# Attention over 13 key tiles in six steps a head instead of seven: the last step multiplies three tiles' values

## What is computed

```python
# wide layer
logits = jnp.einsum('bhqd,bhkd->bhqk', q, k) * scale      # 16 heads, d = 64
probs = jax.nn.softmax(logits + col_bias[None, None, :, :], axis=-1)
out = jnp.einsum('bhqk,bhkd->bhqd', probs, v)
out = out.transpose(0, 2, 1, 3).reshape(B, HW, HEADS * HEAD_DIM) @ Wo + bo + residual
# narrow layer
qg = q.reshape(B, T, N_KV_HEADS, n_rep, HEAD_DIM)         # 4 groups, d = 16
attn = softmax(jnp.einsum('btgrd,bsgd->bgrts', qg, k) * scale)
out = residual + jnp.einsum('bgrts,bsgd->btgrd', attn, v).reshape(B, T, -1) @ wo
```

## Time and profile before

| | |
|---|---|
| runs | median 4529.59 us, 4527.27 to 4530.70 (3 runs) |
| profiled execution | 4529.87 us; its span 4528.1 us, so 1.8 us lie outside the span |
| PE matmuls busy | 4472.1 us, 99% |
| DVE, POOL, ACT busy | 68%, 63%, 51% |
| mean granted clock of PE | 0.991 |
| one wide head | 62 us, and 69 us where an output is projected |
| one narrow head | 39.7 us, and 46 us with a projection |

### The profile page before, as it was taken

How to read it: one execution, slowest core, us unless ns; L and a number is a source line. 1 busy time by engine, 2 the same in 40 slices (tenths; PEclk the granted TensorE clock), 3 DMA queues, 4 the chain that set the end, 5 groups by cost and what they waited for, 6 DMA issues and landing times.

```text
span 4528.1 us, 56837 instructions
## 1 busy us (share of the span) xinstructions
PE 4472.1 (99%) x20621; PEld 2825.6 (62%) x20621; DVE 3067.4 (68%) x5034; ACT 2308.4 (51%) x4123; POOL 2836.3 (63%) x1375
## 2 busy tenths in 40 slices
PE   9999999999999999999999999999999999999999
PEld 8889756666566455555565666666656666666664
DVE  4222567777777687788646777777766677777776
ACT  3322555555555446666654555455555554555453
POOL 0000479888988700111047889888975798889886
PEclk9999999999999989999999999999999999999999
DMA  5565822122212111011151222122216221222120
GB/s 193 181 204 183 276 64 62 44 64 70 66 48 49 36 23 16 12 15 17 57 191 39 63 65 70 45 68 66 56 47 205 64 68 38 64 69 69 45 49 30
DMA packets 125850, 349.61 MB, mean 77 GB/s; under 512 B 29238, under 2 KB 47158, under 8 KB 114619
## 3 DMA queue, kind: packets, MB, share of 16 engines
q1 hardware_dynamic: 125568, 345.98, 28.8%
HBM read 191.38 MB, written 120.31 MB: 69 GB/s over the span
## 4 chain that ended last, share of the span: by engine, by line
PE 94%; DVE 4%; issue 1%; DMA 1%; ACT 0%; POOL 0%; DVEq 0%; SPq 0%; ACTq 0%
PE ST L1098 14%; PE SS L1079 13%; PE ST L1099 12%; PE OA L1109 12%; PE OB L1109 11%; PE ST L1255 5%; PE OA L1263 4%; PE SS L1241 3%; DVE acc L1757 2%; PE OB L1241 1%; PE SS L1118 1%; PE ST L1174 1%; PE ST L1175 1%; PE ST L1176 1%; PE SS L1145 1%; PE SS L1146 1%
## 5 line engine op out<-in xcount | busy, mean ns | idle before, releaser
L958 POOL TENSOR_TENSOR acc<-acc,P 128x1024 f32<-128x1024 f32 x912 | 2215.9, 2461 | 304.2 <-DVE acc L1763 291.1
L1472 ACT ACTIVATE P<-ST 128x512 f32<-128x512 f32 (+1 forms) x2496 | 1464.3, 597 | 1259.8 <-PE ST L1099 1133.6
L1736 DVE TENSOR_REDUCE mpart<-SS 128x1 f32<-128x400 f32 (+1 forms) x3072 | 1629.0, 569 | 666.4 <-PE SS L1079 590.5
L1098 PE MATMUL ST<-QX,KX 128*128 128x512 f32 (+1 forms) x2496 | 1024.7, 411 | 5.6 <-DMA QS<-mrow 3.7
L1099 PE MATMUL ST<-QS,KS 69*128 69x512 f32 (+1 forms) x2496 | 990.2, 397 | 0.0
L1079 PE MATMUL SS<-KS,QS 68*128 68x400 f32 (+1 forms) x3072 | 976.7, 352 | 7.8 <-DVE xacc L1787 2.8
L1079 PEld LDWEIGHTS SS<-KS,QS 68*128 68x128 f32 x3072 | 583.2, 190 | 183.7 <-DVE xacc L1787 26.1
L1098 PEld LDWEIGHTS ST<-QX,KX 128*128 128x128 f32 (+1 forms) x2496 | 464.2, 186 | 361.9 <-issue 274.8
L1109 PE MATMUL OA<-P,Vp 128*64 128x512 f32 (+1 forms) x2496 | 658.3, 606 | 0.0
L1109 PE MATMUL OB<-P,Vp 128*64 128x512 f32 (+1 forms) x2496 | 641.3, 592 | 0.0
L1583 ACT ACTIVATE PG<-ST 128x512 f32<-128x512 f32 (+1 forms) x832 | 425.9, 618 | 202.0 <-PE ST L1255 201.8
(11 more groups left out here) (259 smaller groups left out, 4442.5 us busy)
## 6 DMA issues: line engine op xcount, KB each, us to landing
q_parts<-stq SPq DMA_DIRECT2D x96, 512.0 KB, 5.2
QX<-q_parts SPq DMA_DIRECT2D x96, 512.0 KB, 11.2
KX<-k_parts SPq DMA_DIRECT2D x48, 801.0 KB, 9.3
QS<-q_parts SPq DMA_DIRECT2D x45, 512.0 KB
R<-R SPq DMA_DIRECT2D x360, 64.0 KB, 2.0
v_tiles<-sv SPq DMA_DIRECT2D x24, 832.0 KB, 5.9
Vp<-v_tiles SPq DMA_DIRECT2D x24, 832.0 KB, 7.1
k_parts<-skh SPq DMA_DIRECT2D x48, 400.5 KB, 4.8
```

Of the source, the lines that this page charges most:

```text
L958: gp.tensor_tensor(out, out, P[0:k, slot(H, t), q, :], ALU.add).then_inc(pool_a, 1)
L1098: pe.matmul(bank, KX[H % 2][:, t * 128:t * 128 + k], QX[H % 2][:, q], start=True, stop=False)
L1472: act.activation(P[0:k, slot(H, t), j, :], ST[n % 3][0:k, :], ACT.Exp, scale=SCALE).then_inc(act_p, 1)
L1736: dve.tensor_reduce(mpart[H % 2][:, i // len(KCH), c:c + 1], SS[RING_AT["s", H, i] % 3][:, 0:w], AX.X, ALU.max).then_inc(dve_ss, 1)
```

## The change

One line of the tables. Before, `PV` is 0-1, 2-3, 4-5, 6-7, 8-9, 10-11, 12: seven steps. After, it is 0-1, 2-3, 4-5, 6-7, 8-9, 10-11-12: six steps. So STEPS goes from 7 to 6, ROW_STEP from 5 to 4, and BEFORE_ROW (units ahead of the row's step) from 40 to 32. No instruction of computation is added or dropped.

```diff
-PV = [range(t, min(t + 2, KT)) for t in range(0, KT, 2)]
+PV = [range(t, t + 2) for t in range(0, KT - 3, 2)] + [range(KT - 3, KT)]
 STEPS = len(PV)
 ROW_STEP = STEPS - 2
 BEFORE_ROW = sum(len(PV[g + 1]) for g in range(ROW_STEP)) * JQ
```

## The result

The changed kernel takes 4545.3 us (median of 6 runs, 4539.24 to 4548.1), the kernel before in the same comparison 4528.4 (6 runs). The ratio is 1.0037, with a 95% interval of 1.0027 to 1.0047: slower by 0.37%, 17 us. The forecast was 4536, "no change that can be told, on its slow side"; 4545.3 lies inside its range of 4524 to 4548, but the interval excludes 1, so a change can be told, which the forecast had denied. The profiled execution took 4548.1 us, its span 4546.3, so the two traces differ by 18.2 us.

What follows compares the result with a forecast made beforehand. PE, busy 99% of the span and holding 94% of the chain, was taken as the bound. Wide layers -6.5 and narrow layer +12.8 gave +6.3 us on the profiled 4529.87, forecast 4536, range 4524 to 4548.

Steps and rivals of the forecast that it cites:

- The blocks: Wide heads: each block of values has 0.34 us of overhead, which one block fewer gives back; a block of three takes 5.30.
- the dense steps: First heads: DVE binds; wide steps of 16 S tiles take 7.8 us (+4.45 a layer), narrow ones of 14 6.06 (+4.8).
- the transfer: Narrow head 6: head 8's queries land no earlier, so PE waits 6.3 us for them, net +5.8.
- Rival 1: Only the blocks count and the two waits might hide: -24 us, 4506; chance 0.08.
- rival 2: DVE's ring of S-tile banks binds every narrow 12-unit step: 4548 to 4560, about 4550; chance 0.17.
- Head 15, with two blocks merged, gains 0.2 to 0.3: Last head of each wide layer: merging two blocks makes it 0.2 to 0.3 us shorter.
- Usual wide heads: Wide heads 1 to 13: each gains 0.34 us, 13.3 us over the three layers.
- Nothing new waits there: Wide heads 1 to 13: DVE's 14 S tiles take 7 us beside the 12 units' 8.47, so no new wait.
- Head 6's clock term: Narrow head 6: low clock behind PE's wait costs +1.3 to +3.0 us, taken as 2.2.
- Narrow head 14: It loses S tiles but its units go at ACT's pace; heads 14 and 15 put at 0 (-0.7 to +2).
- Rival 3: Head 6's low clock lasts through the step, three wide first heads lose 1.5 us more each: 4542; chance 0.13.
- A wide layer: Sum of its heads: -4.4 + 4.45 - 1.95 - 0.25 = -2.2 us, the three layers -6.5.

Runs made afterwards that it cites:

- The half reduction: Changed kernel, but DVE takes the maxima of each layer's second head over only half of each S tile's columns: 4528.3 us, ratio 0.9998.
- the early split: Changed kernel, but POOL splits the queries of narrow heads 8 to 15 ahead of head 5's division, not behind it: 4538.0 us, ratio 1.0016.
- the kernel with the step of three at 8 to 10: Six steps as in the changed kernel, but tiles 8-10 form the step of three and 11-12 the last: 4537.4 us, ratio 1.0017 to the kernel before.
- the second five-step kernel: Changed kernel with five steps (tiles 0-1, 2-3, 4-6, 7-9, 10-12), both POOL edits and 12 early S tiles: 4813.4 us, ratio 1.0623.

## Why the prediction was right in its range, and where it was wrong

**The blocks, the dense steps, the transfer: right.** A wide block of three 5.30 us (5.30), 12 units 8.53 (8.47), 16 S tiles 7.74 (7.8), 14 narrow S tiles 6.06 (6.06), 12 narrow units 6.18 (6.2), 12 units without S tiles in head 14 6.1 (6.1 to 6.2), the wait of head 6 6.15 (6.3) and all of head 6 +7.2 (+8.0; +7.3 to +8.4 in the three other kernels that have the wait). The half reduction shows that DVE binds the first heads, and the early split that head 8's queries were the wait. Rival 1 (only blocks count) and rival 2 (the ring in every narrow step) did not come; narrow heads 1 to 5 and 7 to 13 moved by under 0.1 us, but for head 4 (+0.3).

**The step that failed: "Head 15, with two blocks merged, gains 0.2 to 0.3".** It costs 3.2, 3.2 and 4.4 us, 11 us together. The traces differ by 18.2 us where 6.3 was forecast; of these 12 us, head 15 is 11.6, the usual wide heads are 5.7 (below), and head 6, the first heads, the other narrow heads and the last outputs give some 5 back, 2.8 of them by where the low clock lay. I had looked at two of POOL's products (for ACT's splitting and for tile 12's slot) and found 6 and 12 us in hand, but not at the third, the subtraction that the *next* head's output matmul needs. It has 3.5 to 4.5 us in hand in the other pairs and none in heads 14 and 15, where PE waited 1.17 us in the kernel before already. So the 2 us that head 14 gains by its shorter work could not be had: POOL sets the end of head 14. With tiles 11 and 12 taken from POOL they come.

**Terms mis-sized.** Usual wide heads gave -7.6 instead of -13.3. Some 2 us of the difference are the 12 units, which take 8.49 to 8.54 us and not 8.47. The other 3.5 are step 1, which the prediction's "Nothing new waits there" leaves out: it looked at DVE's S tiles beside the 12 units, and not at DVE's additions of tile 1 beside POOL's last ones, whose places move against each other when a head gets shorter. Single heads come out from -1.0 to +0.9 by it. The changed kernel's low clock lies at other places than before: none of the 6.8 us behind layer 0's projection but 3.4 (first head +2.7 instead of +4.3), and 3.4 us in layer 2's last outputs. Head 6's clock term, 2.2, is some 1.3 in the trace (+7.2 less the net wait of 5.9), since the clock rose 3.1 us behind the wait. Narrow head 14 is -1.8 where 0 was forecast; -0.7 to -1.0 of it also stands in kernels with the old narrow table, whose traces lack the low clock that the kernel before has there.

**The verdict.** That 4545.3 lies in the range is in part luck: the upper edge, 4548, was set for rival 2, the ring in the narrow steps, which did not come, and the time got there by head 15, which no rival names. Rival 3, "slower by head 6 and the first heads alone", had the right side and not the right place; its 4542 is near 4545.3, but it got there by a longer low clock in head 6 and slower first heads, of which only layer 3's +5.9 came, by the clock. A wide layer was forecast at -2.2 us and is +1.2 by the median of the kernel with the new table in wide layers alone, +2.4 by its trace.

## What to carry to other kernels

Where PE is 99% busy and a change shortens one stretch of it, follow each operand that PE will need *behind* that stretch to the engine which makes it, and read how long it lay ready before; an engine that works through without a pause ends when it ends. A wait of 2.6 us then cost more than its length here, since the clock was low for 3.4 us or more behind it. An addition on DVE has to be placed against POOL's too: where both add from SBUF at once, both take longer. Work taken from PE's overhead shows only if what is spread over the steps (here DVE's S tiles) keeps its old density; move some of it to a stretch where the other engine is idle. Merging more blocks lost 300 us and more here; by the chains, because products tied to a step's number (the reciprocals, DVE's first additions) then come later than their users.

## What the runs showed of the hardware

- The granted clock was at the 1.2 GHz level around each of the three waits of 2.62 us in head 15 (for 3.4, 3.4 and 6.8 us), behind or around the three of 2.2 us in the kernel with the step of three at 8 to 10 (3.4 us each), and around that of 6.15 us (6.8 us, 3.1 of them behind the wait). It did not fall at the wait of 3.02 us in layer 2's last outputs before, nor at that of 3.01 in layer 3's after.
- A DVE addition of two SBUF operands (128x1024) takes 1.21 us where POOL is quiet, up to 3.4 while POOL adds in the kernels before and after, and up to 7.6 in the second five-step kernel. POOL's own addition takes 2.34 us at least and up to 3.4 beside one of DVE's. DVE's reductions from PSUM keep 0.57.
